# A decoder layer on one core: mLSTM gate tiles of 68 columns, and new orders on all five engines

## The reference

```python
x = layernorm(x + attention(x))        # 16 heads of 16, biased q/k/v/out projections,
                                       # score bias by distance, softmax over 256 keys
x = layernorm(x + mlstm(x, ctx, ctx))  # 4 heads of 64
x = layernorm(x + ffn(x))              # 256 -> 1024 -> 256, silu(gate) * up,
                                       # weights ternary, rows quantised to 8 bit
```

```python
ig, fg = cat(q, k, v) @ igate_kernel + bias, cat(q, k, v) @ fgate_kernel + bias
cs = cumsum(log_sigmoid(fg));  log_D = where(tril, cs - cs.T, -inf) + ig.T
D = exp(log_D - max(log_D));   C = (q @ k.T / 8) * D
h = (C / (max(|sum(C)|, exp(-max(log_D))) + eps)) @ v      # then a norm of each head
```

## Time and profile before

| | |
|---|---|
| median of 3 runs | 827.5 us (827.5 to 833.78) |
| profiled execution, its own time | 828.54 us |
| its span, first to last instruction | 826.8 us |
| TensorE / weight loads busy | 698.1 / 519.6 us (84 / 63%) |
| VectorE, ScalarE, POOL busy | 640.6, 626.0, 491.1 us (77, 76, 59%) |
| mean granted TensorE clock | 0.919 |

### The profile page before, as it was taken

How to read it: one execution, slowest core, us unless ns; L and a number is a source line. 1 busy time by engine, 2 the same in 40 slices (tenths; PEclk the granted TensorE clock), 3 DMA queues, 4 the chain that set the end, 5 groups by cost and what they waited for, 6 DMA issues and landing times.

```text
span 826.8 us, 17709 instructions
## 1 busy us (share of the span) xinstructions
PE 698.1 (84%) x5138; PEld 519.6 (63%) x5168; DVE 640.6 (77%) x2437; ACT 626.0 (76%) x1284; POOL 491.1 (59%) x833
## 2 busy tenths in 40 slices
PE   4279888899898989898989898999989898975642
PEld 3257657577675858585858676777758575743411
DVE  3745454888988888888888988988888889876743
ACT  0427674979898988888888989898989888885622
POOL 2536453657677676776675757676776763735232
PEclk8679996999999999999999999999999999989866
DMA  8876734080605060513224160707060601010100
GB/s 257 152 135 78 94 64 79 2 140 2 143 12 141 15 140 15 119 37 95 61 56 100 35 120 4 152 2 146 10 141 14 123 20 53 14 52 14 39 14 13
DMA packets 63177, 59.97 MB, mean 73 GB/s; under 512 B 6437, under 2 KB 62826, under 8 KB 63082
## 3 DMA queue, kind: packets, MB, share of 16 engines
q1 hardware_dynamic: 63082, 58.84, 34.6%
HBM read 29.39 MB, written 4.26 MB: 41 GB/s over the span
## 4 chain that ended last, share of the span: by engine, by line
PE 69%; ACT 8%; DVE 7%; issue 6%; POOL 5%; DMA 3%; SPq 2%; POOLq 0%; DVEq 0%; ACTq 0%
PE pT L604 12%; PE pO L621 8%; PE pC L661 6%; PE pS L588 6%; PE pC L637 3%; PE pA L747 3%; PE pA L637 3%; PE pC L708 2%; PE pB L708 2%; PE pB L574 2%; SPq L296 2%; ACT L1114 2%; PE pA L695 2%; PE pB L757 1%; PE pC L725 1%
## 5 line engine op out<-in xcount | busy, mean ns | idle before, releaser
L1299 DVE CUSTOM_DVE_ANT_0 sc<-pS,bias 128x256 f32<-128x256 f32 x512 | 200.6, 417 | 39.9 <-PE pS L588 37.6
L604 PE MATMUL pT<-ident,sc 128*128 128x128 f32 x1024 | 155.9, 285 | 35.5 <-ACT pr L946 33.1
L946 ACT ACTIVATE pr<-pT 128x512 f32<-128x512 f32 x256 | 149.0, 596 | 19.2 <-PE pT L604 18.8
L604 PEld LDWEIGHTS pT<-ident,sc 128*128 128x128 f32 x1024 | 123.0, 146 | 59.7 <-issue 52.4
L426 POOL TENSOR_SCALAR sc<-sc,mx 128x256 f32<-128x256 f32 x256 | 122.3, 483 | 59.4 <-DVE mx L1299 56.3
L934 ACT ACTIVATE sc<-sc,mx 128x256 f32<-128x256 f32 x256 | 127.8, 512 | 1.1 <-DVE mx L1299 0.9
L588 PE MATMUL pS<-ks,qs 96*128 96x256 bf16 x512 | 97.5, 278 | 5.5 <-DVE mx L1299 5.5
L478 POOL TENSOR_SCALAR_AFFINE_SELECT mb<-mb 128x256 f32<-128x256 f32 x64 | 26.2, 409 | 98.7 <-ACT mb L973 94.2
L621 PE MATMUL pO<-pr,va 128*32 128x256 f32 x1024 | 76.5, 421 | 0.0
L438 POOL TENSOR_SCALAR hq<-h 128x512 bf16<-128x512 f32 x64 | 38.5, 619 | 55.1 <-ACT h L1122 55.1
L588 PEld LDWEIGHTS pS<-ks,qs 96*128 96x128 bf16 x512 | 44.9, 99 | 37.9 <-DVE mx L1299 12.5
(11 more groups left out here) (236 smaller groups left out, 1790.0 us busy)
## 6 DMA issues: line engine op xcount, KB each, us to landing
qs<-parts SPq DMA_DIRECT2D x96, 128.0 KB, 5.4
ks<-parts SPq DMA_DIRECT2D x96, 128.0 KB, 6.3
mb<-mrows SPq DMA_DIRECT2D x16, 512.0 KB, 6.7
xin<-in_x SPq DMA_DIRECT2D x16, 256.0 KB, 2.8
bias<-in_L_attn_pos_bias SPq DMA_DIRECT2D x4, 1024.0 KB, 21.2
xb<-in_x SPq DMA_DIRECT2D x16, 256.0 KB, 7.0
cx<-in_ctx SPq DMA_DIRECT2D x32, 128.0 KB, 2.2
out<-hq SPq DMA_DIRECT2D x16, 256.0 KB, 5.8
```

Source lines behind the costliest of these rows:

```text
L604: ins = pe.transpose(bank[:, kt * S + t * P:kt * S + t * P + P], sc[:, s % RING, t, kt * P:kt * P + P], ident[:])
L946: act.activation(flat(pr[:, s % RING, :, :]), pT[s % 2][:, :], ACT.Exp, scale=-1.0)\
L1299: dve.tensor_tensor_reduce(out=sc[:, s % RING, t, :], in0=pS[s % 2][:, t * S:t * S + S], in1=bias[:, t, s, ::-1], scale=1.0, scalar=LOW, o ...
```

## The change

The forget gates move from column and row 32 to 64, so that gate_w has 68 columns, and gate_b, gt, sp and am have 68 rows. The product of `mem_gates` then has 68 columns and `exponents_turned` transposes 68 rows. The bodies of all five engines are written anew, and `uses` with them. The counts of instructions in an iteration stay as they were. Cut to its core:

```diff
-        gate_w = sb("gate_w", [P, 6, 64])
+        gate_w = sb("gate_w", [P, 6, 64 + XH])
...
-                sp.dma_start(gate_w[:, :, 32 * part:32 * part + XH],
+                sp.dma_start(gate_w[:, :, 64 * part:64 * part + XH],
...
-                    pe.matmul(bank[0:64, 0:S], gate_w[:, 2 + kt, :], cxT[:, kt, :], start=(kt == 0), stop=False)
+                    pe.matmul(bank[0:64 + XH, 0:S], gate_w[:, 2 + kt, :], cxT[:, kt, :], start=(kt == 0), stop=False)
...
-                    ins = pe.transpose(bank[:, t * P:t * P + 64], am[:, t * P:t * P + P], ident[0:64, 0:64])
+                    ins = pe.transpose(bank[:, t * P:t * P + 64 + XH], am[:, t * P:t * P + P],
+                                       ident[0:64 + XH, 0:64 + XH])
...
-            r = slice(32, 32 + XH)
+            r = slice(64, 64 + XH)
```

More of the change, by code:

```diff
@@ L885, in body @@
                 scores(n, 6, 1 - par)
-                up_proj(f, 2)
+                scores(n, 7, 1 - par)
                 mem_scores(c, 0)
-                scores(n, 7, 1 - par)
+                values(b, 3, par)
                 turned(n, 1)
-                values(b, 3, par)
                 mem_scores(c, 1)
@@ L893, in body @@
                 scores(n, 8, 1 - par)
+                mem_scores(c, 2)
+                mem_values(c, 0)
+                mem_values(c, 1)
                 turned(n, 2)
-                mem_values(c, 0)
-                mem_scores(c, 2)
+                mem_scores(c, 3)
+                mem_values(c, 2)
+                heads_turned(b, 0)
+                heads_turned(b, 1)
+                scores(n, 9, 1 - par)
+                mem_values(c, 3)
+                turned(n, 3)
+                scores(n, 10, 1 - par)
             pe.wait_ge(v_set.sem, V_BC)
@@ L1135, in body @@
                 par = b % 2 if par is None else par
-                n2, n, c, f, e = b + 2, b + 1, b - 1, b - 2, b - 3
+                n2, c, f, e = b + 2, b - 1, b - 2, b - 3
+                negated(c, 15)
+                negated(b, 0)
+                heads_copy(c, 2)
+                exponents(f, par)
+                gate_tanh(e, 3)
+                exponentials(c, 15)
+                negated(b, 1)
+                mem_late(f, 0)
+                mem_weights(f, 0)
+                mem_late(f, 1)
+                mem_weights(f, 1)
+                negated(b, 2)
                 mem_late(f, 2)
-                negated(b, 4)
-                exponentials(b, 1)
+                exponentials(b, 0)
                 mem_weights(f, 2)
                 heads_copy(c, 3)
+                negated(b, 3)
                 mem_late(f, 3)
@@ L1168, in body @@
                 exponentials(b, 8)
+                ctx_copy(c)
+                x1_copy(c)
+                negated(b, 11)
                 x_copy(n2)
-                x1_copy(c)
                 exponentials(b, 9)
-                negated(b, 11)
                 exponentials(b, 10)
@@ new lines, in body @@
+                biased(b, 0, 1)
+                forget_sums(f)
+                biased(b, 1, 0)
+                input_rows(f)
+                biased(b, 1, 1)
+                running_max(f)
+                biased(b, 2, 0)
+                biased(b, 2, 1)
+                biased(b, 3, 0)
+                max_rows(f)
+                gated(e, 0)
+                biased(b, 3, 1)
+                gated_up(e, 0)
+                gated(e, 1)
+                biased(b, 4, 0)
+                gated_up(e, 1)
@@ new lines, in body @@
+                biased(b, 4, 1)
+                gated(e, 2)
+                inner_max(e, 0)
+                biased(b, 5, 0)
+                biased(b, 5, 1)
+                gated_up(e, 2)
+                biased(b, 6, 0)
+                biased(b, 6, 1)
+                biased(b, 7, 0)
+                gated(e, 3)
+                inner_scale(e, 0)
+                mem_weights(f, 0)
+                biased(b, 7, 1)
+                mem_weights(f, 1)
+                gated_up(e, 3)
+                biased(b, 8, 0)
```

290 lines of the change are left out of this document (119 added, 171 removed).

## The result

The changed kernel took 804.72 us (median of 4 runs, 802.02 to 806.7) against 829.65 us for the kernel before in the same session: a ratio of 0.9692, with a 95% interval of 0.9635 to 0.9748. The profiled execution has a span of 805.0 us against 826.8, and a mean granted clock of 0.946 against 0.919.

A forecast was written before the change was run, and what follows sets the result against it. TensorE was taken as the bound, with 39.95 us work, 2.6 standing and 1.5 slow clock an iteration. Going from 43.81 to 42.1 us over 11 iterations saves 18.8, plus 1 elsewhere: 808 us, range 786 to 828, the forecast's own 800 to 817.

The forecast's parts named there:

- The clock: TensorE in the steady state: three short pauses don't bring the clock's fall that one of 2.2 us did, 1.5 us each.
- Rival A: TensorE's clock falls in nearly every iteration all the same: 43.2 us an iteration, 820 us in all; chance 0.20.
- Part 2: ScalarE's order around head 11: earlier exponential takes 1.4 of TensorE's 2.2 us pause before turned(b,13); 0.8 stays.
- Part 3: TensorE from scores(n,0) to scores(n,7): VectorE's work there is late next; cycle with TensorE's way round 42.1 us an iteration.
- Its term for VectorE: VectorE's items from head 0 to head 5, counted in the cycle at 11.7 us.
- Part 1: Gate matmuls with 68 columns in the full 128x128 tile: 0.48 us less TensorE time an iteration, bounds 0 and 0.7.
- The bound 0: Low end for the 68 columns' saving on TensorE: nothing, if entering the next tile costs the same.
- B: VectorE's stretch is shorter or starts earlier, TensorE nears 39.5 us: 40.5 us an iteration, 790 us; chance 0.10.
- Its relative: ScalarE's exponential behind a logarithm needs no table load, so exponentials(b,11) comes 1.28 us earlier; chance 0.02.
- D: Slower: the running maximum's round trip lands late for ScalarE's mem_late; at 4.7 us late, 44.8 an iteration, 842 us; chance 0.08.

The follow-up runs named there:

- the row maximum: Changed kernel with VectorE's inner_max(e, 0) moved from ahead of both halves of head 5 to behind them: 801.4 us, ratio 0.9654; a second time 801.22 us.

## Why the prediction was right

**The time.** 808 us was forecast beside 827.5, a gain of 19.5; the medians differ by 24.9, and 804.7 lies in the forecast's own range. The profiled executions differ by 21.8: 20.3 in twelve iterations, which is 18.6 for eleven, where 18.8 was forecast, and 1.5 in the rest, where 1 was. The other 3 us are a matter of which runs were profiled: 828.54 lies 1.1 below the median before (829.65; it was 827.5 when the forecast was made), and 806.7, the slowest of the four after, lies 2.0 above theirs.

**The clock.** Right in its core. Nine falls fewer at 1.5 us are 13.5 of the 20.3 us, and putting the pause back brought eight of them back. Of the rest, 12 x (42.54 - 42.08) = 5.5 us came at full clock, and 1.3 is not accounted for. Rival A, a fall in nearly every iteration all the same, did not come.

**Part 2** was right: 0.8 us left of the pause forecast, 0.94 measured. The pause before up_proj(f,1) was put at 1.1 and is 0.36, because the scan of running_max took 1.12 us and not 1.53, and VectorE reached gated(f,0) earlier. TensorE was to stand for at least 2.2 us between scores(n,0) and scores(n,7); it stands for 0.38 + 0.94 + 0.36 = 1.7, and none of it is a wait for VectorE's mx, which was forecast. So the waits are not only cut in pieces, they are shorter in sum.

**Part 3** gave the right number with the wrong cycle, and this is the step that failed. "The cycle is: TensorE from scores(n,7) round to scores(n,0) ... Together 42.1 us" is a cycle of 41.44 us at most, as the waits in the run without mem_scaled show. Its term for VectorE was too long: from 407.29 to 418.90 VectorE is busy for 10.99 us after, not 11.7, and with that the prediction's own sum gives 41.4. The iteration of 42.08 is held by the second norm's loop, and a third cycle, over ScalarE's list, has 41.64. The prediction names neither: "I followed the rest of the cycle by the same durations" covers the shared banks, the x1 norm, POOL's split and SyncE's queue, but not the way from head_norm over POOL to the logarithm and on to the tanh. On that way lies a cost that the kernel before did not have, the 1.10 us of "issue" behind head_scale's last multiplication, L1362 (see the last section). So the agreement of 42.08 with 42.1 is luck: a term too long by 0.7 us stood in for a loop that was left out.

**Part 1** was right about TensorE (0.48 forecast, 0.58 between two orders without a long pause) and wrong in putting it into the sum: with 64 columns the changed kernel is no slower. In the kernel before, the columns alone gave 7 us by the median. Its profiled execution, the slowest of the seven, shows 3.7 us of it in the twelve iterations, and they came where the clock had fallen. The bound 0 was in the working; I should have asked which cycle the gates lie on before counting them.

**The rivals.** B's iteration of 40.5 us did not come. Its relative, the rule of the Trainium skill (ScalarE: Activation LUTs, The hidden batching unit) that an exponential behind a logarithm needs no load, did not hold here, and the measurement decides. Of the 33 loads after, fifteen stand in front of an exponential behind the logarithm, as the earlier trace rows said, and sixteen in front of the logarithm. D did not happen: the read of mb was issued at 412.60 and landed 3.6 us later where it had needed 7.7. The stacks' transfers began 1.9 us behind it, not 0.5, which is the likely reason and was not tried. ScalarE's mem_late at 419.47 had 3.3 us in hand. SyncE's timeline and the transfers, after:

```profile
411.33 0.28 SPq L317 DMA_DIRECT2D mrows<-mm  x1
412.60 0.37 SPq L324 DMA_DIRECT2D mb<-mrows  x1
414.53 3.80 SPq L297 DMA_DIRECT2D qs<-parts  x6
...
mb<-mrows SPq DMA_DIRECT2D x1, 512.0 KB, 3.6
```

Open: why filling gained 5.1 us and draining lost 3.6. No run tested either. The runs with two halves moved show that small moves shift the filling by several microseconds.

## What to carry to other kernels

Look for the place where the fastest clock is lost before counting work: here one pause of 2.2 us cost 1.5 us of slow clock behind it, in most iterations. Taking back the new order of a few steps on another engine cost 18 of the 25 us gained. But one of these steps moved in the old orders gained only 3 us: the pause came back as two, and the clock still fell in some iterations. So look at all waits near the place and not only at the longest. When engines are all busy for nine tenths of an iteration, name every loop that closes from one batch to the next and give each its length; a saving counts only on the longest, and a move that lies on several of them, like the row maximum here, is the one to try next. A time that comes out right does not prove the loop: follow the chain of waits all the way round, shorten something that lies on one candidate alone and see whether the time follows.

## What was not expected of the hardware

**A small operation that lasts as long as its neighbour's large one.** head_scale's last multiplication, 128x8 elements, took 0.17 us in the kernel before (sixteen of them, mean 167 ns) and 0.95 us on average after. The VectorE and POOL timelines after, at one of them:

```profile
432.85 0.19 DVE L1360 TENSOR_TENSOR nrm<-nrm,hmv 128x8 f32<-128x8 f32 x1
433.08 1.22 DVE L1362 TENSOR_TENSOR nrm<-nrm 128x8 f32<-128x8 f32 x1
```

```profile
433.00 1.26 POOL L504 TENSOR_TENSOR xb<-xb,bo_bc 128x512 f32<-128x512 f32 x1
```

It starts 0.08 us after POOL's residual_in and ends with it (434.30 and 434.26). The new POOL order puts residual_in just ahead of head_rstd, which waits for this multiplication. The Trainium skill (SBUF — State Buffer, SBUF: two separate sides) calls the port pair that VectorE and GpSimd share an exclusive lock, which whoever starts first holds for the whole instruction; it counts in a VectorE operation with two SBUF inputs against a GpSimd operation that reads SBUF. The two timelines agree. No run moved residual_in away, so that it would shorten the second norm's loop is argued, not shown. It is what I would try next.

**The scan.** running_max's scan, on the same 4x256 elements, took 1.33 us on average before and 0.98 after, and 1.53 and 1.12 in most iterations of the steady state. POOL's split runs beside it in both; what differs is which of its instructions had started, and when. Before, one of 1.31 us had started at 425.17, 0.32 us ahead of the scan, and the scan ended 0.54 us after it. After, one of 0.62 us started at 410.16, 0.03 us ahead, and the scan ended 0.53 us after it. In the one iteration after where the scan was first (494.31, POOL's at 494.37) it took 0.67 us, and POOL's instruction took 1.04 instead of 0.62. No run set this order on purpose.

**A third level of the granted clock.** One profiled execution (the row maximum, again) had 0.95 all through its steady state, neither the full 2.4 GHz nor the 1.2 GHz of the falls, where all others had 1.00 outside the falls. It took 805.98 us, 4.8 more than the median of the same kernel. What grants it is not known.
